# Moving the heads' values product, the query and key projections and some routing work within one Trainium2 kernel's hand-written order

## The chip, the cores and the metric

The kernel runs on one core of a Trainium2 chip. The core has five engines with a queue each: PE (TensorE, matrix products), DVE (VectorE), ACT (ScalarE), POOL (GpSimd) and SP (SyncE, which here issues transfers). Each works through its own instructions in the order in which they are written, and waits on semaphores that other engines or transfers raise. The metric is the device time of one execution in microseconds (us), as the median of several runs. A profiled execution gives a trace: each instruction with its start, its duration and what released it.

## The reference

Eight independent sequences ("bodies", b = 0 to 7) of 1024 tokens with 256 features go through four residual layers: attention with 8 heads of 64 (softmax over keys of a matrix that mixes heads and positions), a gated feed-forward layer whose operands are rounded to 4-bit blocks, attention with 16 heads of 16, and a linear layer with a top-2 mixture of 8 low-rank experts.

```python
def reference(...):
    x = L0_attn_x                                   # (8, 1024, 256)
    x = x + _L0_attn_ref(_layernorm(x), Mq, Mk, Mv)
    x = x + _L0_ffn_ref(_layernorm(x), w_gate, w_up, w_down)
    x = x + _L1_attn_ref(_layernorm(x), w_qkv, b_qkv, g_q, be_q, g_k, be_k, w_proj, b_proj)
    x = x + _L1_ffn_ref(_layernorm(x), W, b, R, A, B)
    return x

def _L1_attn_ref(...):
    qkv = x @ w_qkv + b_qkv                         # 256 -> 3 x 16 heads x 16
    q = _ln(q, g_q, be_q) * HD ** (-0.5)            # each head normalised
    k = _ln(k, g_k, be_k)
    attn = softmax(q k^T); out = attn v
    return out @ w_proj + b_proj
```

## The kernel before

The whole of a body stays in on-chip memory. Matrix products of single precision are made of three half-precision products, a high and a low part of each operand (`mm3`), each of four instructions of 32 columns (`by_columns`). A product is therefore 24 or 48 matmul instructions in the trace.

Two things use the accumulation memory. The attention loops have their own areas, `pS` for scores and `pV` for values. All other products take the next of three banks `pR` in turn (`take`): the fourth product from now needs the bank of this one, and waits until it has been emptied. What goes through the ring in the stretches that matter here: query and key projections of the first attention (`project`, 48 matmuls of 256 columns), output projection of the second attention (`moe_proj`, `wproj`), routing (`moe_rt`, 136 columns of `wmoe`), the heads' queries and keys (`qk`, 24 matmuls of 512 columns on `wqkv`) and values (`v`, 24 of 256 columns), and transposes.

The order on each engine is written by hand. A generator per kind of work (`attn0`, `projections`, `moe_rt`, `heads_qkv`, ...) yields the place, in steps, at which its next piece stands, and `weave` merges the generators of an engine by place. One step is one step of an attention loop. A body takes 129.5 steps: in one half the second attention of body i-1 (`attn1`, 64 steps) runs beside the feed-forward of body i, in the other half the first attention of body i+1 (`attn0`, 64 steps) runs beside the heads' preparation of body i (`heads`, `heads_qkv`, `heads_bias`, `heads_norm`) and the last layer of body i-1 (`moe_*`). The places are the same for bodies 2 to 7 of `attn0`; bodies 0 and 1 are stretched or moved to fill the start.

Step n of the first attention is a chain across engines. PE makes the scores S(n) (L457, 16 matmuls into `pS`), DVE takes their maximum (L1215), ACT the exponential (L897), DVE the reciprocal of its sum (L1232, `rz`), POOL scales the values by it (L1698), and PE multiplies (L558, `pV`). `pS` holds two steps, so S(n) needs the exponential of step n-2. I write max(n) and exp(n) for the maximum and exponential of a step.

Around it, in the same half:

- `project_at(pair, n)` sets the place of projection n (two of queries, two of keys) of token pair 1, 2, 3. PE makes it, ACT takes the high part (L851), DVE the low part, which frees the bank (L1095), and SP spreads the result in transfers (`fill`, L1929). Step 16 x pair of the attention waits for them.
- `qkv_at(t)` sets the heads' products of tile t. On PE `qk` and `v` stand one behind the other. On DVE both evictions do (L1510 for `qk`, L1512 for `v`).
- `heads_norm` squares on ACT (L999), sums on DVE (L1520), computes inverse roots on POOL in three Newton rounds (L1802 to L1815) and multiplies (L1820). PE transposes then, and SP writes the heads out and reads them back in another layout.
- `R_AT` sets the routing products of four tile pairs. DVE reads their logits (L1422), ACT copies the rest and frees the bank (L947). `moe_low` (L1770) and the addition of a bias, L1793 in `heads`, are POOL's.
- `fin_at(n)` sets the first and second half of the preparation of the feed-forward's input: statistics (L1112), an inverse root on POOL (L1716, L1718), normalisation (L1248), rounding (L1129 to L1159), a cast (L1265). Its end is a transposing transfer on SP (L1933), for which the first product on `wgu` waits.
- `ln_at` sets the preparation of body 1 alone (for other bodies it changes nothing).

Of the kernel before, what the change touches and what calls it, by code (L numbers as in the profile page):

```python
# [15 lines left out]
NB = 8  # L16
# [38 lines left out]
def build(nc, a, out):  # L55
    with ExitStack() as ctx:
# [188 lines left out]
        def bank(u):  # L245
            return pR[:, 512 * u.bank:512 * u.bank + 512]
# [36 lines left out]


        P_AT = (2.1, 3.5, 6.5, 8.5)
        R_AT = (19.0, 21.6, 25.2, 28.0)

        def project_at(pair, n):
            return 16 * (pair - 1) + (0, 0, -1)[pair - 1] + 3 * n

        def qkv_at(t):
            return 11 + 9 * (t // 2) + 4 * (t % 2)
# [38 lines left out]

        def ln_at(b, p):

            return .71 * p - 8.3 if b == 1 else p

        def v0_at(b, tp):
            return ln_at(b, 34.3 + 2.2 * tp) if b else 57 + tp
# [5 lines left out]
        def fin_at(n):  # L343


            return -21.5 + .85 * n if n < 20 else 3.3 + .8 * (n - 20)

        def second(b, lane):

# [84 lines left out]
        def _(e):  # L434
# [324 lines left out]
            def heads_qkv(b):  # L759
                for t in range(NT):  # L760
                    yield qkv_at(t) + .4 if b + 1 < NB else qkv_end(t)
                    e.wait_ge(tr_in["H"][t // 4], 16 * (b + 1))
                    if b == 0 and t == 0:
                        e.wait_ge(w_in, 24)
                    for key, at, n in (("qk", 0, 512), ("v", 512, 256)):
                        u = take((key, b, t), two=False)
                        for k in range(2):
                            i = mm3(bank(u)[:, 0:n], columns_of(xT2, k, t), parts(wqkv, k, slice(at, at + n)),
                                    start=(k == 0), stop=(k == 1))
                        i.then_inc(r_full[u.bank], 1)  # L770
# [312 lines left out]
        def _(e):  # L1083
            reg = e.alloc_register("flag_dve")

            def full(key):
                u = ring[key]
                e.wait_ge(r_full[u.bank], u.n)
                return u
# [409 lines left out]
            def heads_bias(b):  # L1499
                for t in range(NT):  # L1500
                    yield qkv_at(t) + 1.15 if b + 1 < NB else qkv_end(t) + .4
                    tp = t // 2
                    if t == 0 and b == 0:
                        e.wait_ge(const_in, 14)
                    if tp > 1 and b + 1 < NB:
                        full(("qkT", b, tp - 2, 1))
                    u = full(("qk", b, t))
                    heads_ = tqn[tp % 2][0] if b + 1 < NB else qke[tp]
                    at = slice(512 * (t % 2), 512 * (t % 2) + 512)
                    e.scalar_tensor_tensor(heads_[:, at], bank(u), 1 / WS, bqkv[:, 0:512], ALU.mult, ALU.add).then_inc(r_free[u.bank], 1)  # L1510
                    u = full(("v", b, t))
                    e.scalar_tensor_tensor(vaug[:, t, :, 0:16], bank(u)[:, 0:256].rearrange("p (h d) -> p h d", d=16), 1 / WS,  # L1512
                                           bqkv[:, 512:768].rearrange("p (h d) -> p h d", d=16), ALU.mult, ALU.add).then_inc(r_free[u.bank], 1)
# [153 lines left out]
        def _(e):  # L1667
# [103 lines left out]

            def moe_low(b, hf=None):
                for tp in range(4) if b < NB - 2 else ():
                    yield 14.4 + tp
                    lows("M", b, tp, xhm_[b])

            def heads(b):
# [8 lines left out]
                    e.tensor_scalar(xhh[:, t, :], xb, ag["H"][:, t, 0:1], rstd["H"][:, t:t + 1], ALU.subtract, ALU.mult).then_inc(xh_in["H"], 1)  # L1786
                for t in range(NT):
                    xb = x[b % 2][:, t, :]
                    yield 11.6 + 0.9 * t
                    e.wait_ge(xh_in["H"], 8 * b + t + 1)  # L1790
                    if b == 0 and t == 0:
                        e.wait_ge(raw1_in, 16 * 11)
                    e.tensor_tensor(xb, xb, bproj[:, :], ALU.add).then_inc(xb1_in, 1)  # L1793
# [429 lines left out]
```

## Time and profile before

| | us |
|---|---|
| median of 3 runs | 2999.08 |
| lowest and highest | 2991.23, 2999.32 |
| the profiled execution, whole | 2993.89 |
| its span in the trace | 2992.1 |
| PE, DVE, ACT, POOL busy | 2591.1, 2109.8, 1962.2, 1190.2 |

The profile page gives the sums of each engine and the costliest groups. It doesn't say where the lost time lies, so the trace is read in stages: which half of a body has idle PE, then which waits end it. All times are from the start of the span. Body 4's first attention, from 1391 to 1564, stands for bodies 2 to 7, whose halves are alike.

### The profile page before, as it was taken

The numbers are of one execution on the slowest core, as the hardware profiler recorded it, in microseconds if no ns is written. First come the engines' busy times: TensorE is split into PE (matmuls) and PEld (weight loads), VectorE is DVE, ScalarE is ACT, GpSimd is POOL, SyncE is SP. The second block draws the span as 40 slices with busy tenths as digits, with TensorE's granted clock in tenths as the row PEclk, the third lists the DMA queues.
The fourth block names the chain that finished last, engine by engine and source line by source line (L and its number), as shares of the span: only waits on it lengthen the run. The fifth ranks groups of instructions, "written<-read, shape, count | busy, mean of one in ns | idle before, by whom it ended". The sixth has DMA issues, their size and how long they took to land.

```text
span 2992.1 us, 115289 instructions
## 1 busy us (share of the span) xinstructions
PE 2591.1 (87%) x50174; PEld 1405.8 (47%) x50174; DVE 2109.8 (71%) x4321; ACT 1962.2 (66%) x3707; POOL 1190.2 (40%) x1677
## 2 busy tenths in 40 slices
PE   4766777999889988899889988899889988899697
PEld 3434554344644456444553456444553446444233
DVE  6778866766778478775778577785788667775433
ACT  2541355776668856787668766787668766687684
POOL 3653156224652166323652155421672246411210
PEclk9987999999999999999999999999999999999798
DMA  4212332324424252323423253152423243222310
GB/s 127 54 27 46 66 70 69 61 48 78 100 64 82 41 113 60 65 63 69 101 74 62 41 92 97 49 85 52 108 63 72 48 85 86 59 66 46 87 30 16
DMA packets 470171, 203.65 MB, mean 68 GB/s; under 512 B 283000, under 2 KB 459648, under 8 KB 469640
## 3 DMA queue, kind: packets, MB, share of 16 engines
q1 hardware_dynamic: 467960, 194.07, 31.3%
q8 instruction: 413, 6.77, 1.0%
q10 hardware_dynamic: 1680, 1.85, 0.2%
q14 instruction: 118, 0.97, 0.1%
HBM read 46.61 MB, written 32.51 MB: 26 GB/s over the span
## 4 chain that ended last, share of the span: by engine, by line
PE 43%; DVE 26%; issue 7%; ACT 7%; SPq 7%; DMA 6%; POOL 3%; DVEq 0%; POOLq 0%; ACTq 0%
PE pR L457 18%; PE pV L688 9%; DVE nmaxa L1215 7%; PE pS L457 6%; PE pS L648 5%; ACT ub L936 5%; PE pV L558 3%; PE pR L467 2%; SPq L1929 2%; SPq L2126 2%; DMA xT<-xhb 2%; SPq L2112 1%; DMA xT<-ua 1%; DVE ua L1118 1%; DMA ua<-ua 1%
## 5 line engine op out<-in xcount | busy, mean ns | idle before, releaser
L936 ACT ACTIVATE ub<-pS 128x512 f32<-128x512 f32 x2048 | 1048.0, 613 | 233.1 <-PE pS L648 232.4
L1215 DVE TENSOR_REDUCE nmaxa<-pS 128x1 f32<-128x1024 f32 x512 | 621.1, 1214 | 280.6 <-PE pS L457 279.2
L897 ACT ACTIVATE ua<-pS,nmaxa 128x1024 f32<-128x1024 f32 x384 | 427.7, 1114 | 457.0 <-DVE nmaxa L1215 454.5
L457 PE MATMUL pS<-ua 128*32 128x512 f16 x8192 | 546.6, 388 | 110.0 <-ACT ua L897 88.5
L688 PE MATMUL pV<-ub,vaug 128*17 128x512 f32 x4096 | 539.8, 600 | 13.4 <-DVE ub L1373 12.6
L1698 POOL TENSOR_TENSOR ua<-ua,rz 128x256 f32<-128x256 f32 x512 | 332.6, 651 | 485.8 <-DVE rz L1232 466.2
L648 PE MATMUL pS<-ub 50*128 50x512 f16 x1920 | 351.5, 385 | 26.6 <-DMA ub<-scr 11.5
L457 PEld LDWEIGHTS pS<-ua 128*32 128x32 f16 x8192 | 212.2, 98 | 280.2 <-ACT ua L897 123.7
L457 PE MATMUL pR<-wgu,xT 128*32 128x352 f16 x6144 | 282.7, 319 | 35.8 <-DMA xT<-ua 15.4
L648 PEld LDWEIGHTS pS<-ub 50*128 50x128 f16 x1920 | 95.8, 93 | 403.8 <-ACT ub L936 332.6
L558 PE MATMUL pV<-ua 128*32 128x128 f32 x6144 | 245.8, 280 | 36.9 <-DVE oTa L1226 22.9
L457 PEld LDWEIGHTS pR<-wgu,xT 128*32 128x32 f16 x6144 | 160.3, 98 | 174.3 <-issue 105.3
L897 ACT ACTIVATE EA<-pS,nmaxa 128x1024 f32<-128x1024 f32 x128 | 142.6, 1114 | 140.8 <-DVE nmaxa L1215 140.8
L558 PEld LDWEIGHTS pV<-ua 128*32 128x32 f32 x6144 | 168.1, 111 | 104.9 <-DVE oTa L1226 38.5
L457 PE MATMUL pR<-wqkv,xT 128*32 128x512 f16 (+1 forms) x3072 | 139.3, 332 | 18.8 <-DMA xT<-xhb 13.2
L1762 POOL CAST xhb<-at_ 128x256 f16<-128x256 f32 x56 | 24.1, 431 | 303.7 <-DVE at_ L1365 255.2
L1743 POOL TENSOR_TENSOR EA<-ua,EA 128x704 f16<-128x704 f32 x28 | 45.5, 1626 | 241.9 <-DVE EA L1324 241.9
L688 PEld LDWEIGHTS pV<-ub,vaug 128*17 128x17 f32 x4096 | 84.9, 96 | 115.0 <-issue 75.4
L457 PE MATMUL pR<-wd,ua 128*32 128x256 f16 x4032 | 130.5, 273 | 4.9 <-DMA ua<-ua 3.0
L457 PEld LDWEIGHTS pR<-wd,ua 128*32 128x32 f16 x4032 | 104.0, 97 | 58.4 <-issue 50.1
L457 PE MATMUL pR<-xT,mq 128*32 128x256 f16 x3072 | 100.9, 283 | 25.6 <-DMA xT<-ua 24.8
L457 PEld LDWEIGHTS pR<-wqkv,xT 128*32 128x32 f16 x3072 | 83.3, 98 | 80.2 <-issue 17.8
(258 smaller groups left out, 4019.0 us busy)
## 6 DMA issues: line engine op xcount, KB each, us to landing
ua<-ua SPq DMA_DIRECT2D x384, 128.0 KB, 2.8
ub<-scr SPq DMA_DIRECT2D x264, 64.0 KB, 2.9
scr<-ub SPq DMA_DIRECT2D x30, 512.0 KB, 3.6
x<-in_L_attn_x SPq DMA_DIRECT2D x8, 1024.0 KB, 6.1
between<-x SPq DMA_DIRECT2D x7, 1024.0 KB, 5.9
ub<-between SPq DMA_DIRECT2D x7, 1024.0 KB, 6.1
out<-ub SPq DMA_DIRECT2D x7, 1024.0 KB, 5.5
ub<-scr SPq DMA_DIRECT2D x192, 32.0 KB, 1.9
```

Source lines behind the costliest of these rows:

```text
L457: i = e.matmul(dst[j:j + 32], w[:, j:j + 32], m, start=start, stop=stop)
L467: return e.matmul(dst, src, ident[0:n, 0:n], is_transpose=True)
L558: i = e.matmul(pV[32 * jl:32 * jl + 32, 128 * jg:128 * jg + 128], vs[n % 4][:, j, :], EA[n % 4][:, 128 * j:128 * j + 128], start=(c == 0 a ...
L648: e.matmul(pS[:, 512 * hl:512 * hl + 512], kk_[row:row + 50, o, 128 * c:128 * c + 128], q[row:row + 50, o, 512 * qh:512 * qh + 512]).then_ ...
L688: i = e.matmul(pV[32 * hl:32 * hl + 17, :], vaug[:, c, 4 * hg + hl, :], EB[(4 * n + hl) % 8], start=(c == 0), stop=(c == 7))
L897: e.activation(EA[n % 4], pS[:, 1024 * (n % 2):1024 * (n % 2) + 1024], ACT.Exp, bias=nmaxa[:, n % 32:n % 32 + 1], accum_out=zz[:, n % 8:n ...
L936: e.activation(EB[(4 * n + hl) % 8], pS[:, 512 * hl:512 * hl + 512], ACT.Exp).then_inc(e1_in, 1)
L1215: e.tensor_reduce(nmaxa[:, n % 32:n % 32 + 1], pS[:, 1024 * (n % 2):1024 * (n % 2) + 1024], AXX, ALU.max, negate=True).then_inc(max0_in, 1)
L1698: e.tensor_tensor(vs[m % 4], vv[:, :, 32 * c:32 * c + 32], rz[:, c:c + 1].unsqueeze(2).to_broadcast([128, 8, 32]), ALU.mult).then_inc(vs_i ...
L1743: e.tensor_tensor(pair[:, 1, 0:FI], h_[b > 0][t % 2][:, 0:FI], pair[:, 0, 0:FI], ALU.subtract).then_inc(hlh_in, 1)
L1929: e.dma_start(dst[r0:r0 + 64, par::2, o:o + 256], sh[64 * par:64 * par + 64, w, l, :, :]).then_inc(fill0[pair % 2], 16)
L2126: e.dma_start(dst[at:at + 16, o:o + 2, :], scr[b % 2, w_, l, 64 * hg:64 * hg + 64, :].rearrange("(h p d) n -> p d h n", p=2, d=16)[par]).t ...
```

## The change

Only places are changed, and two `yield` lines are added. Nothing is computed otherwise.

```diff
-        R_AT = (19.0, 21.6, 25.2, 28.0)
+        R_AT = (19.0, 21.6, 25.2, 27.0)
...
-            return 16 * (pair - 1) + (0, 0, -1)[pair - 1] + 3 * n
+            return 16 * (pair - 1) + (0.0, 0, -1)[pair - 1] + 3.5 * n
...
-            return .71 * p - 8.3 if b == 1 else p
+            return 0.71 * p - 7.8 if b == 1 else p
...
-            return -21.5 + .85 * n if n < 20 else 3.3 + .8 * (n - 20)
+            return -22.0 + 0.85 * n if n < 20 else 3.3 + .8 * (n - 20)
...
                     for key, at, n in (("qk", 0, 512), ("v", 512, 256)):
+                        if key == "v" and b + 1 < NB:
+                            yield qkv_at(t) + .4 + .6
                         u = take((key, b, t), two=False)
...
+                    if b + 1 < NB:
+                        yield qkv_at(t) + 1.15 + .6
                     u = full(("v", b, t))
                     e.scalar_tensor_tensor(vaug[:, t, :, 0:16], bank(u)[:, 0:256] ...
...
             def moe_low(b, hf=None):
                 for tp in range(4) if b < NB - 2 else ():
-                    yield 14.4 + tp
+                    yield 14.7 + tp
...
-                    yield 11.6 + 0.9 * t
+                    yield 10.6 + 0.9 * t
```

So: `v` and its eviction come 0.6 of a step behind `qk`; projections of a pair stand 3.5 steps apart, the last one 1.5 steps later than before; the last routing pair comes one step sooner; the first half of the feed-forward's input preparation half a step sooner; the bias additions on POOL one step sooner; body 1's early preparation 0.5 step later. Since lines are added, lines below 766 have numbers higher by two in the changed kernel, those below 1510 by four.

PE in body 4's first attention, steps 20 to 24. `pS` are the scores of a step, `pV` the values product, `mk` a key projection, `wmoe` routing, `ident,ub` the heads' transposes. Before:

```order
L457 MATMUL pS<-ua 32x512 x16
L558 MATMUL pV<-ua 32x128 x8
L467 MATMUL pR<-ident,oTa 128x128 x2
L457 MATMUL pR<-wqkv,xT 32x512 x24
L457 MATMUL pR<-wqkv,xT 32x256 x24
L558 MATMUL pV<-ua 32x128 x8
L457 MATMUL pS<-ua 32x512 x16
L457 MATMUL pR<-wmoe,xT 32x136 x48
L558 MATMUL pV<-ua 32x128 x8
L457 MATMUL pS<-ua 32x512 x16
L457 MATMUL pR<-xT,mk 32x256 x48
L558 MATMUL pV<-EA,ua 32x128 x8
```

and now:

```order
L457 MATMUL pS<-ua 32x512 x16
L558 MATMUL pV<-ua 32x128 x8
L467 MATMUL pR<-ident,oTa 128x128 x2
L457 MATMUL pR<-wqkv,xT 32x512 x24
L558 MATMUL pV<-ua 32x128 x8
L457 MATMUL pS<-ua 32x512 x16
L457 MATMUL pR<-wqkv,xT 32x256 x24
L457 MATMUL pR<-wmoe,xT 32x136 x48
L558 MATMUL pV<-ua 32x128 x8
L457 MATMUL pS<-ua 32x512 x16
L558 MATMUL pV<-EA,ua 32x128 x8
L457 MATMUL pS<-ua 32x512 x16
```

The values product of 24 matmuls stands behind the scores of step 21, and the key projection has gone behind those of step 23.

PE in the same body, from the scores of step 25 to those of step 28. Before:

```order
L457 MATMUL pS<-ua 32x512 x16
L457 MATMUL pR<-wmoe,xT 32x136 x48
L457 MATMUL pR<-xT,mk 32x256 x48
L558 MATMUL pV<-ua 32x128 x8
L457 MATMUL pS<-ua 32x512 x16
L558 MATMUL pV<-EA,ua 32x128 x8
L457 MATMUL pS<-ua 32x512 x32
```

and now:

```order
L457 MATMUL pS<-ua 32x512 x16
L457 MATMUL pR<-wqkv,xT 32x256 x24
L457 MATMUL pR<-wmoe,xT 32x136 x48
L558 MATMUL pV<-ua 32x128 x8
L457 MATMUL pS<-ua 32x512 x16
L558 MATMUL pV<-EA,ua 32x128 x8
L457 MATMUL pR<-xT,mk 32x256 x48
L457 MATMUL pS<-ua 32x512 x16
L457 MATMUL pR<-wmoe,xT 32x136 x48
L457 MATMUL pS<-ua 32x512 x16
```

The key projection stands behind the scores of step 26, and the last routing pair, which stood behind the scores of step 28, comes ahead of them.

DVE around the maxima of steps 43 and 44 (`nmaxa`). `vaug` is the eviction of `v`, `stF` and `agF` are the statistics of the feed-forward's input. Before:

```order
L1215 TENSOR_REDUCE nmaxa<-pS 128x1
L1226 COPY oTa<-pV 128x256
L1510 SCALAR_TENSOR_TENSOR ub<-pR,bqkv 128x512
L1512 SCALAR_TENSOR_TENSOR vaug<-pR,bqkv 128x16x16
L1112 BN_STATS stF<-x 128x6
L1114 BN_AGGR agF<-stF 128x2
L1232 RECIPROCAL rz<-zz 128x1
L1109 SCALAR_TENSOR_TENSOR ub<-pR,ub 128x256
L1215 TENSOR_REDUCE nmaxa<-pS 128x1
```

and now, with two of the statistics already ahead of the first row:

```order
L1217 TENSOR_REDUCE nmaxa<-pS 128x1
L1228 COPY oTa<-pV 128x256
L1512 SCALAR_TENSOR_TENSOR ub<-pR,bqkv 128x512
L1234 RECIPROCAL rz<-zz 128x1
L1111 SCALAR_TENSOR_TENSOR ub<-pR,ub 128x256
L1114 BN_STATS stF<-x 128x6
L1116 BN_AGGR agF<-stF 128x2
L1516 SCALAR_TENSOR_TENSOR vaug<-pR,bqkv 128x16x16
L1217 TENSOR_REDUCE nmaxa<-pS 128x1
```

The reciprocal no longer has the eviction of `v` and a statistics pair ahead of it.

## Rows read from the trace of the kernel before

**Rows 1.** Windows: us, busy us of PE, PEld, DVE, ACT, POOL, PEclk, DMA share, GB/s.

```profile
235.00:322.00 87.00, 49.90 (x1202) 35.90 (x1198) 74.32 (x142) 9.61 (x19) 23.75 (x17) 0.81 0.31 56
322.00:530.00 208.00, 157.26 (x3530) 102.38 (x3526) 145.82 (x255) 101.54 (x169) 102.75 (x162) 0.91 0.31 68
...
1391.00:1564.00 173.00, 148.98 (x3726) 100.35 (x3722) 139.49 (x295) 102.95 (x179) 111.24 (x173) 0.99 0.40 89
1564.00:1736.00 172.00, 166.21 (x2558) 71.40 (x2554) 114.08 (x218) 140.68 (x280) 34.89 (x35) 1.00 0.31 57
```

**Rows 2.** Waits in 1391 to 1563: engine and line, releaser: total us, times, longest.

```profile
PEld pV L558 <- POOL ua L1698: 6.7, 9, 1.2
PE pS L457 <- ACT ua L897: 8.4, 12, 1.6
```

**Rows 3.** Timeline, opening of body 4: start, us, engine, line [idle before, releaser].

```profile
1411.89 1.49 PE L457 MATMUL pR<-wproj,xT 128*32 128x256 f16 x48 [0.63 <-DVE ua L1095]
...
1419.86 2.13 PE L457 MATMUL pR<-wqkv,xT 128*32 128x512 f16 x48 [0.93 <-DMA xT<-xhb]
1420.18 3.56 SPq L1929 DMA_DIRECT2D ua<-ua  x4
...
1422.91 1.22 DVE L1215 TENSOR_REDUCE nmaxa<-pS 128x1 f32<-128x1024 f32 x1 [0.61 <-PE pS L457]
...
1424.05 0.73 DVE L1118 TENSOR_SCALAR ub<-ub,agM,rstdM 128x256 f32<-128x256 f32 x2
...
1429.59 1.73 DVE L1118 TENSOR_SCALAR ub<-ub,agM,rstdM 128x256 f32<-128x256 f32 x2
...
1432.38 1.04 PE L457 MATMUL pS<-ua 128*32 128x512 f16 x16
```

**Rows 4.** Windows, two stretches of the same half: columns as in group 1.

```profile
1413.00:1440.00 27.00, 22.17 (x554) 14.26 (x546) 25.87 (x51) 16.91 (x29) 21.19 (x26) 1.00 0.42 80
...
1512.00:1563.00 51.00, 40.70 (x946) 25.24 (x942) 42.38 (x78) 29.99 (x50) 33.78 (x48) 0.99 0.28 72
```

**Rows 5.** The chain of work, 1440 to 1475: start, us, engine and line.

```profile
1452.62 1.31 PE pR L457 x48
...
1458.49 1.95 PE pR L457 x48
```

**Rows 6.** Timeline, steps 21 to 28.

```profile
1450.04 0.68 DVE L1510 SCALAR_TENSOR_TENSOR ub<-pR,bqkv 128x512 f32<-128x512 f32 x1
...
1450.78 0.54 PE L457 MATMUL pR<-wmoe,xT 128*32 128x136 f16 x24 [1.57 <-DVE ub L1510]
...
1466.86 1.22 DVE L1215 TENSOR_REDUCE nmaxa<-pS 128x1 f32<-128x1024 f32 x1 [2.24 <-PE pS L457]
...
1469.22 0.43 ACT L947 ACTIVATE xhb<-pR 128x128 f32<-128x128 f32 x2
1469.38 1.05 PE L457 MATMUL pS<-ua 128*32 128x512 f16 x16 [1.27 <-ACT ua L897]
```

**Rows 7.** Timeline, steps 30 to 33.

```profile
1477.55 1.22 DVE L1215 TENSOR_REDUCE nmaxa<-pS 128x1 f32<-128x1024 f32 x1 [2.08 <-PE pS L457]
...
1484.59 2.13 PE L457 MATMUL pR<-wqkv,xT 128*32 128x512 f16 x48 [0.68 <-DVE ua L1095]
```

**Rows 8.** Timeline, steps 43 to 50.

```profile
1512.69 1.23 DVE L1215 TENSOR_REDUCE nmaxa<-pS 128x1 f32<-128x1024 f32 x1 [1.42 <-PE pS L457]
...
1518.27 0.41 DVE L1112 BATCH_NORM_STATS2 stF<-x 128x6 f32<-128x256 f32 x1
...
1522.85 0.24 POOL L1716 TENSOR_SCALAR varF<-agF 128x4 f32<-128x4 f32 x1
1523.17 1.04 POOL L1718 TENSOR_TENSOR rstdF<-varF,half 128x4 f32<-128x4 f32 x1
...
1529.34 1.21 DVE L1129 TENSOR_REDUCE amx<-ua 128x64 f32<-128x1024 f32 x1
...
1530.42 1.09 PE L467 MATMUL pR<-ident,ub 128*128 128x128 f32 x8 [0.53 <-POOL ub L1820]
```

## The prediction

> **What bounds the kernel now.** I read the windows by halves of a body first [rows 1]. In the half with the second attention (1564 to 1736) PE is busy 166.21 of 172 us. Little can be won there, and the change moves almost nothing there. In the half with the first attention (1391 to 1564) PE is busy 148.98 of 173 us: 24 us without a matmul. That half occurs six times alike (bodies 2 to 7), and nearly every moved instruction stands in it. The clock is at 0.99 and 1.00 in both, so at its upper level, and the waits cost themselves and no clock.
>
> Next the waits of that half [rows 2]. PE's scores wait for the exponential 12 times, 8.4 us in all, and weight loads of the values product wait for POOL's scaling 9 times, 6.7 us. So PE isn't short of work but sits at the head of an in-order queue while the chain scores, maximum, exponential, reciprocal, scaling is late. It is late where PE put long products ahead of S(n): DVE is idle 2.24 us before max(26), 2.08 before max(30), 1.42 before max(43), each time waiting for scores [rows 6 to 8]. Elsewhere DVE is the full engine: 25.87 busy of 27 us between 1413 and 1440 [rows 4]. A reordering wins where it fills an idle stretch of the engine that is full right after, and wins nothing where DVE or a transfer sets the pace.
>
> **The change, part by part.** The two products that move cost 1.31 us (48 matmuls, a projection) and 1.95 us (`qk` and `v` together), of which `v` has a third of the columns, 0.65 us [rows 5]. No instruction is added or removed, so the sum is only of waits.
>
> *Steps 0 to 18.* `v` of tile 0 goes behind S(12), which comes 0.65 us sooner; DVE stood idle 0.61 us before max(12) [rows 3]. The two projections beside the output projection move too, so PE's 0.63 us wait for a bank goes, but right after it `wqkv` waits 0.93 us for the transposed heads [rows 3], which arrive when DVE and POOL have made them: that 0.63 us moves into this wait and is worth nothing. DVE is full from there on [rows 4], so a lead of 0.61 is kept. Against it stand POOL's bias additions one step sooner. They now stand ahead of a scaling that a values product waits for; and of the four normalisation pairs L1118, one took 0.73 us and another 1.73 us [rows 3]. Bounds -0.95 to +0.7; I take -0.5, near the 0.61.
>
> What a page says of that pair: the 1.73 us pair ran while POOL was adding, the 0.73 us one while POOL was idle. The Trainium skill, SBUF — State Buffer, Who interferes with whom, has it that VectorE and GpSimd hold a shared port exclusively and the second to issue is fully blocked. The trace agrees with that reading (1.73 beside 0.73). By that rule, with the additions a step sooner, the first pair would meet one as well: 1.0 us per body, 6 in all, and the sum below would be 2985 instead of 2979.
>
> *Steps 19 to 28.* At step 21 the second routing product needs the bank that `qk` filled. It waits 1.57 us, until DVE, after max(21), has evicted it (L1510) [rows 6]. Since S(21) now comes before `v`, max(21) and the eviction come 0.65 us sooner, while PE arrives at the same time: 0.65 is won. At step 25 the same wait appears, but there a key projection has come in front (ahead of S(24)), and I count its gain as used up. Then S(26) no longer has a projection before it: 1.31 us sooner, with DVE idle 2.24 us before max(26) [rows 6]. So exp(26) is sooner and the 1.27 us wait of S(28) goes. In its place the last routing pair stands ahead of S(28) and needs banks that ACT's copies (L947) free only after exp(26). They started at 1469.22, beside the S(28) of before [rows 6], and come as much sooner as exp(26). Bounds 0 to -1.92 (0.65 and 1.27); I take -1.3, the first in full and half of the second.
>
> *Steps 29 to 43.* S(30) is 0.65 sooner, where DVE is idle 2.08 and then full up to `wqkv` of step 33, which waited 0.68 us for DVE to free a bank [rows 7]. That wait falls to 0.03. Bounds 0 to -0.68; I take -0.65, since both ends of the wait are in the rows. Later projections go behind scores where PE has no wait; nothing.
>
> *Steps 43 to 63.* This third has the most idle PE: 40.70 busy of 51 us [rows 4]. S(43) is 0.65 sooner, before which DVE is idle 1.42, and one statistics piece (0.41 and more) moves into that idle time [rows 8]. So the reciprocal of step 44 is 0.65 to about 1.2 us sooner. But POOL's inverse root (0.24 and 1.04 us) now stands ahead of the first Newton round, and so ahead of the scaling that it followed; it delays that by about 1.3. The half-step lead of the rounding work is worth nothing by itself: the product on `wgu` waits for SP's queue of head transfers, which starts with POOL's L1820 [rows 8]. Bounds +1.3 to -1.2; I take -0.6.
>
> The sum of a body: 0.5 + 1.3 + 0.65 + 0.6 = 3.05 us, six times 18.3.
>
> *The start.* Body 1's half (322 to 530) has PE busy 157.26 of 208 us [rows 1]. The same deferral of `v` acts there, twice where PE is short, so 1.3 us; its places are stretched, so -4 to +4. `ln_at` delays work of body 1 where DVE is busy 74.32 of 87 us [rows 1]: DVE has the same work in another order, so nothing, 3 us either way. `moe_low` at 14.7 instead of 14.4 moves no instruction.
>
> Together 19.6 us. The profiled execution took 2993.9 us, so 2974.3; the median of the runs shown is 5.2 us above it, at 2999.1. From the median: **2979.5 us**.
>
> **The rivals.**
>
> *Waits change places.* Only step 33's wait and half of step 21's go; the other leads end at a full DVE, or at the transfers that `wqkv` and `wgu` wait for. For it speaks that DVE is 96% busy for 27 us in a row [rows 4]. About 1 us per body: 2993.
>
> *All leads are kept.* 0.95 + 1.92 + 0.68 + 1.2 = 4.75 per body, 28.5, and 1.3 at the start: 2969. For it: every one of these leads begins in a stretch in which the rows show DVE idle. Against: one engine's lead must pass three others.
>
> *Slower: the last third pays.* The rounding work stands half a step sooner on DVE, so its long instructions (L1129 1.21 us, and others) come ahead of a reciprocal or a maximum that they followed, and POOL's root (1.28) ahead of a scaling. Each delays a values product, for which PE already waits 6.7 us per half [rows 2], and PE's later scores behind it. Two of the former and the root are 3.7 us; with half of them absorbed by DVE's idle 1.42 and the like, and with nothing kept of the earlier leads, 2 us per body, 12 in all: 3011. It decides if the lead at step 43 is under about 1.3 us, the size of the root.
>
> *A transfer comes too late.* The last key projection of pair 1 is evicted about one step later, 2.6 us (173 us by 65.5 steps); SP issued its transfers at 1420.18 for 3.56 us, and S(16), which needs them, was at 1432.38 [rows 3]. The slack is 8.6 us to the last issue before, some 6 now, against the landing. If S(16) waits for them after all, 1 to 2.6 us are lost per body: about 2990.
>
> **How the numbers follow.** Chances: forecast 0.43, all leads kept 0.20, waits change places 0.22, slower 0.11, late transfer 0.04. Two runs of this kernel can be told apart from about 0.3%, 9 us: faster is below 2990.1, slower above 3008.1. Faster takes the first two cases and a little of the others, 0.65; slower 0.10; the rest 0.25. The range reaches from the full sum with 5 us of the start's uncertainty (2964) to past the third case, with half of the slower one left out: 3002.
>
> **What would show it.** In the changed profile the routing product of step 21 waits about 0.9 us instead of 1.57; DVE's idle time before the maxima of steps 12, 26, 30 and 43 is 0.6 to 1.3 us shorter; the waits of S(28) and of `wqkv` at step 33 are gone or short; PE's busy time is unchanged and a first-attention half takes about 169.5 instead of 172.5 us, with the other halves at 171. The forecast is wrong if those leads show but the half is as long as before (the second case), if values products of steps 44 to 60 wait for POOL longer than 6.7 us in all (slower), or if scores wait for the spread projections at steps 16, 32 or 48.

## The result, and the profile after

The changed kernel takes 2961.26 us in the median of 4 runs (2956.37 to 2964.51), the kernel before 2995.89 beside it: a ratio of 0.9885, 95% interval 0.9869 to 0.9902. It is faster by 34.6 us (29 to 39), where 19.6 were forecast, and its time lies below the forecast range (2964 to 3002). A second comparison gave 0.9886 (0.9869 to 0.9903). The forecast started from a median of 2999.08, 3.2 us above the one measured beside the changed kernel, so of the 18.2 us between 2979.5 and 2961.26 some 3 are the base and 15.0 the gain. Its profiled execution has a span of 2960.9 us, 31.2 less than before. PE is busy 2590.0 us, as before (2591.1), so waits went and no work did.

The windows of the same halves (columns as in [rows 1]):

```profile
231.00:316.00 85.00, 48.00 (x1213) 34.35 (x1207) 74.28 (x142) 9.84 (x20) 22.67 (x17) 0.82 0.31 60
316.00:521.00 205.00, 157.96 (x3538) 102.86 (x3534) 145.81 (x255) 101.56 (x169) 103.98 (x162) 0.92 0.30 68
1374.00:1544.00 170.00, 150.03 (x3733) 102.03 (x3726) 140.00 (x296) 103.67 (x180) 111.73 (x173) 0.98 0.40 90
1544.00:1714.00 170.00, 164.54 (x2534) 70.63 (x2534) 114.05 (x218) 140.30 (x279) 35.06 (x35) 1.00 0.31 57
```

Body 4's first attention takes 170 instead of 173 us; PE's 24 idle us are 20. Its waits, to be held against [rows 2]:

```profile
PE pS L457 <- ACT ua L899: 8.0, 8, 2.3
PEld pV L558 <- POOL ua L1702: 4.0, 5, 1.4
```

The waits for POOL's scaling fell from 6.7 to 4.0 us. Those of the scores are fewer, but the longest has grown from 1.6 to 2.3. The timeline of the opening says where (against [rows 3]). The first line is the heads' `qk` product of step 11, the second the first normalisation pair, the third S(15):

```profile
1401.86 1.48 PE L457 MATMUL pR<-wqkv,xT 128*32 128x512 f16 x24 [0.73 <-DMA xT<-xhb]
...
1405.40 1.02 DVE L1120 TENSOR_SCALAR ub<-ub,agM,rstdM 128x256 f32<-128x256 f32 x2
...
1411.15 1.88 PE L457 MATMUL pS<-ua 128*32 128x512 f16 x16 [2.27 <-ACT ua L899]
...
1412.81 2.37 PE L457 MATMUL pR<-wqkv,xT 128*32 128x512 f16 x24
```

The lead of step 12 ends in a wait of 2.27 us before the scores of step 15, which need the exponential of step 13. The matmuls behind it are slow. The window of that stretch shows the granted clock at 0.57 (eighth figure), that is at its lower level, 1.2 of 2.4 GHz, for most of it:

```profile
1411.20:1415.20 4.00, 4.00 (x48) 1.75 (x52) 4.00 (x7) 2.76 (x5) 3.63 (x6) 0.57 0.36 69
```

In the kernel before, PE stood idle twice in the same place, 2.00 us in sum:

```profile
1427.22 0.64 PE L558 MATMUL pV<-EA,ua 128*32 128x128 f32 x16 [0.75 <-POOL ua L1698]
1429.12 1.05 PE L457 MATMUL pS<-ua 128*32 128x512 f16 x16 [1.25 <-ACT ua L897]
```

The timeline from step 21 on, against [rows 6 to 8]:

```profile
1432.61 0.68 DVE L1512 SCALAR_TENSOR_TENSOR ub<-pR,bqkv 128x512 f32<-128x512 f32 x1
...
1433.34 0.54 PE L457 MATMUL pR<-wmoe,xT 128*32 128x136 f16 x24 [0.92 <-DVE ub L1512]
...
1445.82 0.54 PE L457 MATMUL pR<-wmoe,xT 128*32 128x136 f16 x24 [0.92 <-DVE ub L1512]
...
1447.71 1.23 DVE L1217 TENSOR_REDUCE nmaxa<-pS 128x1 f32<-128x1024 f32 x1 [0.93 <-PE pS L457]
...
1451.12 1.04 PE L457 MATMUL pS<-ua 128*32 128x512 f16 x16
...
1457.10 1.23 DVE L1217 TENSOR_REDUCE nmaxa<-pS 128x1 f32<-128x1024 f32 x1 [1.11 <-PE pS L457]
...
1464.13 1.48 PE L457 MATMUL pR<-wqkv,xT 128*32 128x512 f16 x24
...
1501.40 1.05 PE L457 MATMUL pS<-ua 128*32 128x512 f16 x16 [1.48 <-ACT ua L899]
...
1503.34 1.08 PE L558 MATMUL pV<-ua 128*32 128x128 f32 x16 [0.89 <-POOL ua L1702]
```

Both routing products wait 0.92 us instead of 1.57 and 1.56; DVE's idle time is 0.93 instead of 2.24 before max(26) and 1.11 instead of 2.08 before max(30), and before max(12) and max(43), where it was 0.61 and 1.42, there is none; S(28) (1451.12) and step 33's product on `wqkv` (1464.13) don't wait. In the last third waits stand in new places (the last two lines: S(47), and a values product behind it).

I worked out two sums from these traces. A step's time is the start of its maximum on DVE. Over bodies 2 to 7 a first attention is 2.84 us shorter on average (3.48 in the second profiled execution, `changed_again` below). And the start, up to the end of body 0's second attention, is 11.5 us shorter (11.3). The two make nearly the whole: 6 x 2.84 is 17.0, with 11.5 it is 28.5 of 31.2. So the forecast's 18.3 for the bodies is about right, and its 1.3 for the start is far too small.

One trace's start is uncertain. Up to the same point `l_only` (below) was 9.0 us shorter by its trace and `v_product_only` 4.1, and `l_only`'s measured times can't be told from the kernel before. Body 0's second attention, which no edit touches, was about 2 us shorter in most traces and unchanged in three. So how the start divides rests on the measured times of the kernels below, and the traces say where to look. Two stretches came out alike in both executions: step 36 to 48 of body 0 (39.6 us before) is 5.0 and 4.9 us shorter, step 24 to 44 of body 1 (65.7) 5.9 and 6.0. They are not the net gain: steps 8 to 16 of body 1 are 3.5 us longer in both.

### The profile page after: what moved, and what is told of

Read it like the earlier page. It is cut to its first block, busy times and chain, and to the rows that moved or that the text cites. A ratio compares the mean times of both kernels' runs of the same rounds, so it can differ in the third digit from the quotient of the medians.

```text
span 2960.9 us, 115289 instructions
## 1 busy us (share of the span) xinstructions
PE 2590.0 (87%) x50174; PEld 1409.4 (48%) x50174; DVE 2114.2 (71%) x4321; ACT 1963.4 (66%) x3707; POOL 1189.8 (40%) x1677
## 4 chain that ended last, share of the span: by engine, by line
PE 43%; DVE 28%; issue 8%; ACT 7%; SPq 6%; DMA 5%; POOL 4%; DVEq 0%; POOLq 0%; ACTq 0%
PE pR L457 18%; PE pV L688 9%; DVE nmaxa L1217 7%; PE pS L457 6%; PE pS L648 5%; ACT ub L938 5%; PE pV L558 3%; PE pR L467 2%; SPq L1933 2%; SPq L2130 1%; DMA xT<-xhb 1%; DVE ua L1120 1%; SPq L2116 1%; DMA ua<-ua 1%; DVE ua L1097 1%
## 5 line engine op out<-in xcount | busy, mean ns | idle before, releaser
L688 PE MATMUL pV<-ub,vaug 128*17 128x512 f32 x4096 | 540.2, 601 | 13.6 <-DVE ub L1375 12.9
L1702 POOL TENSOR_TENSOR ua<-ua,rz 128x256 f32<-128x256 f32 x512 | 322.4, 631 | 449.4 <-DVE rz L1234 437.5
L648 PE MATMUL pS<-ub 50*128 50x512 f16 x1920 | 352.4, 386 | 27.4 <-DMA ub<-scr 11.5
L457 PE MATMUL pR<-wqkv,xT 128*32 128x512 f16 (+1 forms) x3072 | 149.8, 334 | 10.8 <-DMA xT<-xhb 10.4
L457 PEld LDWEIGHTS pR<-wqkv,xT 128*32 128x32 f16 x3072 | 83.2, 98 | 68.3 <-DMA xT<-xhb 13.6
```

The source lines that it names most:

```text
L457: i = e.matmul(dst[j:j + 32], w[:, j:j + 32], m, start=start, stop=stop)
L648: e.matmul(pS[:, 512 * hl:512 * hl + 512], kk_[row:row + 50, o, 128 * c:128 * c + 128], q[row:row + 50, o, 512 * qh:512 * qh + 512]).then_ ...
L688: i = e.matmul(pV[32 * hl:32 * hl + 17, :], vaug[:, c, 4 * hg + hl, :], EB[(4 * n + hl) % 8], start=(c == 0), stop=(c == 7))
L1702: e.tensor_tensor(vs[m % 4], vv[:, :, 32 * c:32 * c + 32], rz[:, c:c + 1].unsqueeze(2).to_broadcast([128, 8, 32]), ALU.mult).then_inc(vs_i ...
```

## The experiments

All are made from the kernel before by some of the edits, unless the text says from the changed kernel. "Body 0" and "body 1" are, if nothing else is said, these two stretches, and "bodies" is the mean saving of a first attention in bodies 2 to 7 by the trace.

### The parts alone

`v_only`: the values product and its eviction 0.6 of a step behind.

```diff
+                        if key == "v" and b + 1 < NB:
+                            yield qkv_at(t) + .4 + .6
...
+                    if b + 1 < NB:
+                        yield qkv_at(t) + 1.15 + .6
```

> Only the heads' values product and its eviction come 0.6 of a step behind queries and keys. Theory 1 (the prediction's: scores that come 0.65 us sooner are kept wherever DVE was idle before their maximum): per body of the first attention 0.6 us by step 18, 0.65 at step 21, 0.65 at step 33, 0.6 at step 43, so 2.5 us, six times 15, and 1 to 2 in body 1: 2979 to 2982. Theory 2 (the projections do the work, the values product alone only moves waits): under 1 us per body, 2990 to 2996. Body 0 has no values product in its attention, so both expect nothing up to 235 us of the span.

Measured 0.9945 (0.9925 to 0.9965), 16.5 us, the first theory. Bodies 2.26 us; body 0 is 2.5 us longer, body 1 0.1 shorter. No instruction of body 0's attention is moved by this edit, so its 2.5 us are chance: by so much one trace can be off in such a stretch.

`j_only`: the projections, in all bodies.

```diff
-            return 16 * (pair - 1) + (0, 0, -1)[pair - 1] + 3 * n
+            return 16 * (pair - 1) + (0, 0, -1)[pair - 1] + 3.5 * n
```

> Only the projections of a pair stand 3.5 steps apart instead of 3. Theory 1: the scores of step 26 lose the projection ahead of them and the wait of S(28), 1.27 us, goes, the rest unchanged: 1 to 1.5 us per body, 6 to 9 us. Theory 2 (the projections do the work): the 2.4 us that the whole change wins between steps 20 and 28 are here alone, 14 us. For the start: the whole change wins 4 us in body 0's attention, where only this edit and the half-step lead of the input preparation act. If this edit does it, 4 us are gone before 235 us of the span; if the other does, none.

Measured 0.9986 (0.9967 to 1.0004). By the trace body 0 is 4.6 and body 1 5.9 us shorter, but the whole of body 0's attention only 0.8 and that of body 1's 2.9: steps 8 to 16 of body 1 are 3.4 us longer. The later bodies win 1.5 us by step 26 and have given all but 0.15 back by step 43. The second theory's 14 us fell. The first's 1 to 1.5 us per body show in the trace up to step 30 (1.2) and are lost again, and the 4 us by 235 us are 0.6.

`f_only` and `l_only`: `fin_at` at -22.0, and `ln_at` at -7.8. `b_only`: POOL's bias additions at 10.6.

> Only the first half of the feed-forward's input preparation comes half a step sooner. The prediction gave it nothing in bodies 2 to 7 but let it cost up to 1.3 us there by POOL's inverse root ahead of the Newton rounds: then 2996 to 3004. If the lead of 4 us at the end of body 0's attention, or the 2.4 us in body 0's feed-forward, is this edit's, the time is 2 to 6 us shorter by 320 us of the span and not after that.

> Only the early preparation of body 1 comes half a step later. The prediction gave it nothing, 3 us either way, since DVE does the same work in another order. The whole change wins 2.4 us between the end of body 0's attention and the start of body 1's. If this edit does it, those 2.4 us show here, and nothing behind them changes.

> Only the projection's bias additions of the head rows one step sooner on POOL (10.6 instead of 11.6). Theory 1 (they fill idle POOL time and bring the transposed heads sooner): 0.2 to 0.5 us per body at steps 10 to 12, ratio 0.999. Theory 2 (they collide with the normalisation pairs on VectorE or delay POOL's scaling): 0.5 to 1.0 us lost per body, ratio 1.001 to 1.002.

Measured 0.9998 (0.9975 to 1.0022), 0.9993 (0.9970 to 1.0016) and 1.0008 (0.9994 to 1.0022): each alone can't be told from nothing. The last routing pair's earlier place was not tried alone.

`no_v`: the changed kernel without the two `yield` lines of `v_only`.

> The changed kernel with the values product and its eviction where they were; all other edits made. Theory 1 (the edits add up, by stages): v alone measured 0.9945, so this run is at 0.9885/0.9945 = 0.994, 2975 us, with the start about 10 us shorter in its trace and the steady bodies 0.3 to 0.7 us shorter each. Theory 2 (the other edits gain only beside v): at 0.998, the sum of the three parts measured alone.

Measured 0.9968 (0.9955 to 0.9981), 9.6 us; bodies 0.36 us, body 0 4.7, body 1 5.9. The trace is as the first theory had it, but the measured ratio is not: its interval holds the second theory's 0.998 and not 0.994. Whether v and the rest are worth more together isn't clear: 0.9945 x 0.9968 is 0.9913, the whole 0.9885, and the intervals just meet. By the traces v makes nearly all of the bodies' gain, and the start's comes with the other edits.

### The start

`spacing_first`: 3.5 steps in bodies 0 and 1 alone.

```diff
-        def project_at(pair, n):
+        def project_at(pair, n, b):
...
-            return 16 * (pair - 1) + (0, 0, -1)[pair - 1] + 3 * n
+            return 16 * (pair - 1) + (0, 0, -1)[pair - 1] + (3.5 if b <= 1 else 3) * n
```

> The kernel before with projections 3.5 steps apart in bodies 0 and 1 alone. Theory 1 (the spacing's gain is all at the start, where the steps are stretched): its trace is 4.7 us shorter from step 36 to step 48 of body 0 and 5.9 us shorter from step 24 to step 44 of body 1, with 1 to 3 us lost elsewhere in these bodies, and bodies 2 to 7 as before; ratio 0.997, about 8 us. Theory 2 (the start's gain in single traces is chance of that execution or is handed back before body 2): ratio 0.999 to 1.000.

Measured 0.9971 (0.9957 to 0.9985), 8.7 us: the first theory. Body 0 is 4.9 us shorter, body 1 7.9, the later bodies 0.1. The whole of body 0's attention is 0.4 us shorter and that of body 1's 7.5, by this one trace.

Why, the timelines of body 1, step 28, tell. SP is one queue for the query and key transfers (`ua<-ua`, eight and then four of a pair), weight loads and the transposes of the heads. Before:

```profile
397.60 15.03 SPq L1929 DMA_DIRECT2D ua<-ua  x12
412.67 3.33 SPq L1933 DMA_TRANSPOSE xT<-xhb  x1
...
418.26 3.90 PE L457 MATMUL pR<-wqkv,xT 128*32 128x512 f16 x48 [5.30 <-DMA xT<-xhb]
```

and with the spacing:

```profile
396.82 5.91 SPq L1929 DMA_DIRECT2D ua<-ua  x8
408.92 1.98 SPq L1933 DMA_TRANSPOSE xT<-xhb  x1
411.49 3.42 SPq L1929 DMA_DIRECT2D ua<-ua  x4
...
413.63 1.90 PE L457 MATMUL pR<-wqkv,xT 128*32 128x512 f16 x16 [2.18 <-DMA xT<-xhb]
```

The last four key transfers now stand behind the transpose, and PE waits 2.18 instead of 5.30 us. In body 1 the kernel stretches a place p to -30 + p x 94/64, and the order hung on a hair: SP's place for the key transfers was -30 + 26.6 x 94/64 = 9.07, the transpose's is 9.1; with 3.5 steps it is 11.27. Two kernels change SP's order alone, in body 1 and in body 0.

`sp_swap` (body 1) and `sp_body0`:

```diff
-                        yield project_at(pair, 2 * w + 1) + 1.6
+                        yield project_at(pair, 2 * w + 1) + (1.7 if b == 1 and pair == 2 and w == 1 else 1.6)
...
+                        yield project_at(pair, 2 * w + 1) + (3.1 if b == 0 and pair == 3 and w == 1 else 1.6)
```

> One edit: in body 1 alone SP issues the last four key transfers of projection pair 2 behind the first head transpose (xT from xhb) instead of ahead of it. All other engines keep their order. Theory 1 (the gain at the start comes from SP's queue): in body 1 the product on wqkv at step 28, which waited 5.30 us for that transpose, waits 2.2 us, the stretch from step 24 to step 44 of body 1 is 3 to 6 us shorter (it was 65.7), the second attention and all later bodies are unchanged, and the whole is 3 to 6 us faster: ratio 0.998 to 0.999. Theory 2 (the gain there comes from the later projections on TensorE, and SP's order only followed): the wait stays at 5 us or moves to the scores of step 32, the stretch is unchanged, ratio 1.000.

> The kernel before with one edit: in body 0 SP issues the last four key transfers of pair 3 behind the second load of w_down instead of ahead of it. All other engines keep their order. Theory 1 (SP's queue): VectorE's wait of 1.76 us for w_down (L1569, at 167.16) goes, TensorE's wait of 4.22 us for the copy behind it falls to 2.5 us, step 36 to 48 of body 0 is 2 to 5 us shorter, and the whole 0.999 or a little under. Theory 2 (TensorE's projections): the wait for w_down goes but another takes its place, the stretch is within 1 us of before, ratio 1.000.

Measured 0.9995 (0.9984 to 1.0006) and 1.0003 (0.9990 to 1.0016). The timeline of `sp_swap`:

```profile
408.80 2.02 SPq L1933 DMA_TRANSPOSE xT<-xhb  x1
410.92 3.13 SPq L1929 DMA_DIRECT2D ua<-ua  x4
...
414.95 4.03 PE L457 MATMUL pR<-wqkv,xT 128*32 128x512 f16 x48 [3.96 <-DMA xT<-xhb]
```

The queue alone takes 1.3 us off the wait, not 3.1, and the stretch is 0.8 us shorter. The rest goes with the engines' order: with the projection behind the scores, DVE converts the heads (L1101) 4.8 us after max(24) instead of 6.2, in `spacing_first` against both other traces. The order in body 0 is the same story. Before, DVE waits for a weight load that stands behind key transfers, and PE behind DVE:

```profile
167.16 0.89 DVE L1569 TENSOR_REDUCE amw<-ub 128x44 f32<-128x704 f32 x1 [1.76 <-DMA ub<-in_L_ffn_w_down]
...
168.65 1.08 PE L558 MATMUL pV<-ua 128*32 128x128 f32 x16 [4.22 <-DVE oTa L1226]
```

and in `sp_body0`:

```profile
167.58 0.88 DVE L1569 TENSOR_REDUCE amw<-ub 128x44 f32<-128x704 f32 x1
...
169.30 1.08 PE L558 MATMUL pV<-ua 128*32 128x128 f32 x16 [2.60 <-DVE oTa L1226]
```

The wait fell from 4.22 to 2.60 us as the first theory had it, but 1.9 us of lead at step 46 were gone at step 48. So neither theory holds whole: both local waits become shorter with SP's order, and little of it is kept without TensorE's.

`ln_fin`: `ln_at` and `fin_at` together. `ln_fin_sp`: these with both orders of SP.

> The kernel before with the shift of body 1's normalisation and projections (ln_at) and that of body 0's feed-forward rounding work (fin_at), and nothing else. Theory 1 (both reach waits of body 0 that the spacing also reaches): body 0's attention 3 to 6 us shorter in the trace (without v it was 6.5), its feed-forward stage about 2 us shorter, body 1's unchanged; ratio 0.998. Theory 2 (what the no-spacing kernel gained in body 0 was v's or chance): ratio 0.9992, body 0 within 2 us of before.

> As ln_fin, and SP's queue in the order that the spacing gives it, in body 0 (second load of w_down ahead of the last key transfers) and in body 1 (first head transpose ahead of them); TensorE keeps its order. Theory 1 (with the waits behind them also gone, the queue is the spacing's whole part): body 1's stretch from step 24 to 44 is 4 to 6 us shorter, 0.995 to 0.997. Theory 2 (as with the queue alone: the local wait falls by 1.3 to 1.7 us and the next wait takes it): within 1.5 us of ln_fin, 0.998.

Measured 0.9979 (0.9965 to 0.9993), 6.3 us, and 0.9977 (0.9960 to 0.9993). Together the two edits are worth something. By the trace body 0's attention is 3.5 us shorter and its feed-forward 2.0, the first theory, though `v_only`, with nothing moved in that attention, was 4.6 us longer there. SP's order adds nothing beside them either, so what the spacing brings needs PE's order too.

`changed_no_spacing`: the changed kernel with 3 steps.

> The changed kernel with the projections 3 steps apart as before; all other edits made. Theory 1 (edits add up, the spacing is worth 9 to 10 us at the start and nothing later): 0.9885 + 0.0030 = 0.9915, 2967 us. Theory 2 (the spacing gains beside v more than alone, since v hides what the third pair gives back at step 39): 0.9925 to 0.994, 2970 to 2974 us.

Measured 0.9899 (0.9878 to 0.9920), the first theory's 0.9915 rather than the second's; bodies 2.53 us, body 0 3.6, body 1 0.3. The interval reaches below the changed kernel's 0.9885, so in the whole the spacing's worth is not shown. The start gains in body 0 without the spacing too, by which `ln_at` and `fin_at` are the likely ones; body 1's 5.9 us, and the 3.5 us that its steps 8 to 16 give back, are the spacing's.

### The eviction

`v_product_only`: as `v_only`, but with DVE's eviction where it was (the second `yield` left out).

> The kernel before with the values product 0.6 of a step later on TensorE, but its eviction left where it was on VectorE. Theory 1 (the gain of v is VectorE's: the maximum comes sooner because the product no longer stands ahead of the scores): now VectorE waits for the product before it takes the maximum, about 0.65 + 0.40 us after the scores end where before it was 0.65 + 0 by then, so 0.4 us lost at most of the 8 tiles of 7 bodies, up to 20 us: ratio 1.003 to 1.007. Theory 2 (what counts is only that scores come sooner on TensorE): 0.9945 as with both.

Measured 0.9927 (0.9908 to 0.9945), bodies 3.41 us. The first theory fell badly. By the traces the gain isn't smaller but larger, by 1.15 us per body; by the measured times the two kernels can't be told apart. What I had overlooked: between S(12)'s end and max(13) DVE has other work, behind which the product is done in time. The timelines show what the deferred eviction costs. `v_only`, step 12 and 13:

```profile
1422.64 0.40 DVE L1512 SCALAR_TENSOR_TENSOR vaug<-pR,bqkv 128x256 f32<-128x256 f32 x1
1422.86 0.61 POOL L1698 TENSOR_TENSOR ua<-ua,rz 128x256 f32<-128x256 f32 x1 [1.62 <-PE pV L558]
1422.96 1.06 DVE L1101 TENSOR_TENSOR xhb<-ub,xhb 128x512 f16<-128x512 f32 x1
...
1423.94 1.21 DVE L1215 TENSOR_REDUCE nmaxa<-pS 128x1 f32<-128x1024 f32 x1
...
1426.45 1.76 PE L457 MATMUL pS<-ua 128*32 128x512 f16 x16 [2.27 <-ACT ua L897]
```

and `v_product_only`:

```profile
1414.25 0.66 DVE L1101 TENSOR_TENSOR xhb<-ub,xhb 128x512 f16<-128x512 f32 x1
1414.47 0.92 POOL L1698 TENSOR_TENSOR ua<-ua,rz 128x256 f32<-128x256 f32 x1 [1.95 <-DVE rz L1232]
1414.84 1.21 DVE L1215 TENSOR_REDUCE nmaxa<-pS 128x1 f32<-128x1024 f32 x1
...
1417.34 1.05 PE L457 MATMUL pS<-ua 128*32 128x512 f16 x16 [1.25 <-ACT ua L897]
```

In the first POOL's scaling starts 0.10 us ahead of L1101, which then takes 1.06 us; in the second L1101 starts 0.22 us ahead and takes 0.66, and the scaling takes 0.92 instead of 0.61. It is so in all six bodies of either kernel. From max(12) to max(13) it is 4.39 us in the first and 3.97 in the second, 0.42 less. The Trainium skill, SBUF — State Buffer, Who interferes with whom, says that two SBUF inputs on VectorE contend with GpSimd's reads and that the order of issue decides who is blocked; the trace agrees, either engine lost 0.3 to 0.4 us by starting second.

Then the clock. The windows from S(15) on (the lines with the waits of 2.27 and 1.25 us), `v_only` and `v_product_only`:

```profile
1426.40:1430.00 3.60, 3.55 (x36) 1.50 (x40) 3.60 (x6) 2.36 (x5) 3.23 (x5) 0.53 0.44 82
```

```profile
1417.30:1420.00 2.70, 2.66 (x60) 1.59 (x64) 2.70 (x5) 2.21 (x4) 2.34 (x4) 1.00 0.58 109
```

After the wait of 2.27 us the clock is at its lower level, after 1.25 us it is not. That is body 4; the length of this one wait doesn't decide it. I counted the bodies 2 to 7 of all twenty traces by PE's idle time from the end of S(14) to S(15). `v_only` and the other kernels that defer both have one wait of 2.0 to 2.3 us: in 16 of 35 such halves the 40 matmuls behind it took 3.2 to 4.0 us instead of 2.34. The eleven kernels without v, the one before among them, have the same 2.0 us in sum or more, as 0.75 and 1.26 us: 22 of 66. Where the product alone is deferred the sum is mostly 1.4 to 1.7 us, and none of the 18 halves with such a sum was slow. So deferring both didn't bring the slow clock, and isn't shown to make it more frequent; deferring the product alone went without it.

`changed_early_evict`: the changed kernel without the eviction's `yield`.

> The changed kernel with the eviction of v on VectorE where it was before (the product stays deferred on TensorE). Theory 1 (with the eviction deferred the reciprocal of step 12 comes 0.3 us sooner, so that POOL's scaling starts ahead of L1101 and lengthens it from 0.66 to 1.06 us, and the wait at step 14 is 0.8 us longer): 0.7 to 0.9 us per body, 4 to 6 us in all against the changed kernel: ratio 0.9865 to 0.987. Theory 2 (beside the other edits, POOL's additions a step sooner among them, the collision is there whatever the eviction does): 0.9885.

Measured 0.9891 (0.9873 to 0.9909): no gain. S(15)'s wait is back at 1.26 us in all six bodies, but the values product ahead of it waits 0.34 us on average for POOL's scaling, and S(19) 1.56 instead of 1.20 (1.44 in `changed_again`); bodies 3.13 us, between the changed kernel's 2.84 and 3.48. The cost that is plain beside v alone isn't there in the whole, the second theory, though not for the reason it gave.

### What the third pair and the routing still cost

`changed_again` is the changed kernel. `all_pair3`, from the changed kernel:

```diff
-            return 16 * (pair - 1) + (0, 0, -1)[pair - 1] + 3.5 * n
+            return 16 * (pair - 1) + (0, 0, -1)[pair - 1] + (3.5 if pair < 3 or b <= 1 else 3) * n
```

`pair3_route` adds

```diff
-        R_AT = (19.0, 21.6, 25.2, 27.0)
+        R_AT = (19.0, 22.1, 26.1, 27.0)
```

and `combined` is `pair3_route` with the eviction not deferred.

> The changed kernel itself, for a comparison on one chip with the kernels beside it. Ratio 0.9885 as first measured (0.987 to 0.990 by every theory).

> The changed kernel, but in bodies 2 to 7 the third pair's four projections stand 3 steps apart again, as before (bodies 0 and 1 keep 3.5). In the run with the spacing alone, 1.2 us per body was won by step 30 and 1.0 of it given back at steps 40 to 42. Theory 1 (the third pair's wider spacing gives it back): steps 30 to 43 win 0.6 to 1.0 us per body, 4 to 6 us in all: 2956, ratio 0.987 to the kernel before. Theory 2 (it is given back whatever the pair's spacing, since the next wait is another engine's): the same as the changed kernel, 0.9885, within 2 us.

> all_pair3 with the second and third routing pairs (24 + 24 matmuls on wmoe) 0.5 and 0.9 of a step later, so that they stand behind the scores of steps 22 and 26 instead of ahead of them; the changed kernel waits 0.92 us in the middle of each of them for VectorE's eviction of qk. Theory 1 (those two waits are on the path): both go, 1.0 to 1.8 us per body are won, 6 to 11 us against all_pair3: ratio 0.985 to 0.986. Theory 2 (VectorE's or ScalarE's queue is the bound there, since copies and maxima of the routing come later too): the wait shows up at the scores or the transposes of steps 23 to 28, ratio 0.988, or up to 0.990 where the last routing pair now waits for banks.

> The changed kernel with the eviction where it was, the third pair's projections 3 steps apart in bodies 2 to 7, and the second and third routing pairs 0.5 and 0.9 of a step later. By the stages of the traces each is worth something (4 to 6, 5, 0 to 4 us). Theory 1 (they add up): 2949 to 2953 us, ratio 0.985 to 0.986. Theory 2 (the next waits take it): as the changed kernel, 0.988.

Measured 0.9886 (0.9869 to 0.9903), 0.9882 (0.9866 to 0.9898), 0.9883 (0.9865 to 0.9901) and 0.9867 (0.9848 to 0.9886). By the traces the bodies win 2.84 and 3.48 us in the changed kernel, 3.86 in `all_pair3` (between step 30 and 43 it wins 0.7 us where the changed kernel loses 0.2, as its first theory had it), 4.36 in `pair3_route` and 4.73 in `combined`. In `pair3_route` both 0.92 us waits are gone, but on average 1.07 us stand before the last routing pair (0.27 in the changed kernel) and 1.10 before the key projection at step 26 (0.48). By the measured times only `combined` seems better than the changed kernel, by about 0.2%, 5 to 6 us, and the intervals overlap: not shown.

Those two averages hide what they are made of. PE stands still for 2.7 to 3.7 us in four of the six bodies and hardly at all in the others, and the trace names no releaser. In body 4 of `pair3_route` it stops after 39 of a projection's 48 matmuls:

```profile
1447.39 1.29 PE L457 MATMUL pR<-xT,mk 128*32 128x256 f16 x39
1451.58 0.50 PE L457 MATMUL pR<-xT,mk 128*32 128x256 f16 x9 [2.89 <-issue]
```

Each trace has some such stops, 67 of over 0.8 us in the twenty, from the first attention of body 2 to that of body 7. Each of the 67 ended 1.2 to 1.6 us after a 16 KB packet of the DMA queue of kind "instruction" had landed, of which there is one in about 7 us. So PE was most likely waiting for its own next instructions. In the first attentions of bodies 2 to 7 these stops sum to 13.6 us in `pair3_route` and 13.2 in `combined`, 4.7 in the changed kernel and 0 in its second execution. That is about as much as the two executions' 2.84 and 3.48 differ by (4.7 by six is 0.8). And in `pair3_route` a body had won 6.1 us by step 26 and 2.5 by step 28: of these 3.6 us the stops are 2.1. So the routing edit's gain is not refuted by the next wait of its chain alone.

## Why the forecast was too small

**Steps 0 to 18**, forecast 0.5 us per body, were 0.07 (0.0 in the second execution). The 0.63 us before `wproj` moved on, but not into the wait for the transposed heads: the waits on `wqkv` sum to 1.36 us against 1.31, and S(7), which didn't wait before, waits 0.65. The lead at step 12 was there and ended in S(15)'s wait. The first pair L1118 took 1.02 instead of 0.73 us, 0.3 and not the 1.0 that the shared port could have cost, and in `v_only`, where the additions stay, it took 1.02 in this body as well. The price of 1.0 was read off the wrong neighbour: the two instructions of the 1.73 us pair took 0.56 and 1.25, and the long one ran beside POOL's L1770, not beside a bias addition (L1793, 0.73 us):

```profile
1429.95 1.22 POOL L1770 TENSOR_TENSOR xhb<-ub,xhb 128x512 f16<-128x512 f32 x1
```

The additions alone (`b_only`) cost nothing that can be measured.

**Steps 19 to 30**, forecast 1.3 and 0.65, were about 3.0. Both 0.65 us leads at the routing products were kept, where I had counted the second as used up; that is the term's error, in the forecast's disfavour by 0.65 us. S(28) and step 33 lost their waits as said. `no_v` and `v_only` each give 1.8 us from step 18 to 30, and the changed kernel 3.0 and, in its second execution, 3.6.

**Steps 30 to 63**, forecast 0.6 for the last third, were nothing. PE's waits from step 44 on sum to 7.8 us before and 7.9 after, averaged over six bodies: there they changed places. Between step 30 and 43 0.2 us were lost, and `all_pair3` shows the reason: the third pair, later by up to one and a half steps, costs 0.9 us there. In sum the bodies came to 2.84 and 3.48 us against 3.05 forecast. The mechanism (leads that begin in DVE's idle stretches) was right, but that the number is right is luck: the forecast had 1.0 us too little in the middle and 1.2 too much before and behind it.

**The start** is the step that failed: "the same deferral of `v` acts there, twice where PE is short, so 1.3 us". `v_only` wins nothing in its two stretches. What acts there is the spacing (8.7 us alone, 4.5 to 12.9) and `ln_at` with `fin_at` (6.3 us together, 2.1 to 10.5): 15.0 in sum, and about 11 by the traces of the whole, where I took 1.3. The ratios of v, the spacing at the start and `ln_fin` multiply to 0.9895, against 0.9885 measured: with these three the gain is accounted for within its interval. It is no proof that they add up, since all edits but v (`no_v`) measured 9.6 us and not 15. I gave the projections a price only in body 4, where PE's order is the whole matter, and called `ln_at` the same work in another order. Body 0 and 1 have what body 4 hasn't: body 0's weight loads stand in SP's queue, and in body 1 twelve query and key transfers stood there ahead of the heads' transpose, since its places are stretched. My bound of 4 us for the start was taken from no row of that stretch. That [rows 1] show PE with 51 idle us in body 1's half was the sign to read it.

**The rivals.** "All leads are kept" (2969) was nearest in time and for the wrong reason. "Waits change places" is what the last third did. The late transfer and the slower last third didn't occur.

What stays open: how the start's gain divides between the spacing and the other two edits (in body 0's stretch the spacing alone has 4.9, the other two alone 1.7, all but the spacing 3.6), whether v and the rest are worth more together than each alone, what the last routing pair's place does alone, and whether `combined` beats the changed kernel.

## What to carry to other kernels

Cost a moved step in every stage in which it moves, above all in the first bodies, where queues also carry loads: read what the one DMA queue holds there and which of two entries with nearly equal places comes first, and don't expect that order alone to win. Read a gain at the start from measured times, since one trace can be off there by as much as the gain. A product moved behind the scores pays if the vector engine is idle before their maximum; its eviction need not move with it, and should be tried apart.

## What the runs showed of the hardware

- The TensorE clock can fall after PE has stood idle for about 2 us inside a busy stretch, in one wait or in two close together. Between S(14) and S(15) of bodies 2 to 7 PE was idle for 2.0 us or more in 102 halves of the twenty traces, and in 38 of them the next 40 matmuls took 3.2 to 4.0 us instead of 2.34, at a granted clock of 0.53 to 0.69 over 3.6 us. In the 18 halves with 1.4 to 1.7 us they never did. The same kernel shows both outcomes in its six bodies.
- PE stood still for 0.8 to 3.7 us with no releaser named in 67 places of the twenty traces, and each time a 16 KB packet of the instruction queue had landed 1.2 to 1.6 us before it went on. One reordering of PE's instructions had 13.6 us of this in six bodies, the kernel before 2.5.
- With a DVE and a POOL instruction, each with two inputs, that start 0.1 to 0.2 us apart the second pays: 1.06 instead of 0.66 us on DVE (`v_only`), or 0.92 instead of 0.61 on POOL (`v_product_only`), in all six bodies.
